# Attention and expert layer on one core: dividing by the softmax sums in the transposed layout, gate columns beside the values' weights, queries and keys laid out by direct copies

## The reference

```python
x = L0_attn_x                                   # (4, 512, 256) float32
# attention, 16 heads of 16, causal, no bias
qkv = (x @ w_qkv).reshape(b, s, 3, 16, 16)
q, k, v = qkv[:, :, 0] / 4, qkv[:, :, 1], qkv[:, :, 2]
scores = where(causal, einsum('bqhd,bkhd->bhqk', q, k), -1e10)
out = einsum('bhqk,bkhd->bqhd', softmax(scores), v).reshape(b, s, 256)
x = layernorm(x + out @ w_out)
# 32 experts, top 4 of each token
w4, i4 = top_k(softmax(x @ gate), 4); w4 = w4 / w4.sum()
for each token and each of its experts e:
    g, u = split(x @ gate_up[e])                # 2 x 96
    y += w4[e] * ((u * silu(g)) @ down[e])      # 96 -> 256
x = layernorm(x + y)
```

## Time and profile before

| what | us |
|---|---|
| median of the runs | 477.55 |
| lowest, highest | 477.39, 483.26 |
| span of the profiled execution | 420.8 |
| PE busy in the span | 377.7 (90%) |
| DVE busy | 287.1 (68%) |
| ACT busy | 242.4 (58%) |
| POOL busy | 235.4 (56%) |

### The profile page before, as it was taken

The page is one execution under the profiler, slowest core; times in us unless marked ns, Lnnn a source line. Parts: engine busy times, 40 slices in busy tenths (PEclk is TensorE's granted clock), DMA queues, the critical chain, the costliest instruction groups (busy, mean ns, idle before and its releaser), DMA issues.

```text
span 420.8 us, 10405 instructions
## 1 busy us (share of the span) xinstructions
PE 377.7 (90%) x2894; PEld 223.1 (53%) x2894; DVE 287.1 (68%) x1009; ACT 242.4 (58%) x534; POOL 235.4 (56%) x374
## 2 busy tenths in 40 slices
PE   5979999999999999997989899988999999989780
PEld 2526554444565445653444466665676777665230
DVE  1157767887879789889799489763666666643562
ACT  2431566667555776556857447562666666556842
POOL 5422144444223888227872855777777766646762
PEclk9999999999999999999999999996999999999987
DMA  4858555646751282649547435636655554429693
GB/s 137 261 192 231 172 165 173 189 136 209 213 164 29 90 277 91 190 144 276 176 149 224 138 123 149 189 132 195 188 175 169 165 158 145 129 69 369 235 375 118
DMA packets 54071, 74.78 MB, mean 178 GB/s; under 512 B 9842, under 2 KB 45308, under 8 KB 52480
## 3 DMA queue, kind: packets, MB, share of 16 engines
q1 hardware_dynamic: 46832, 56.93, 45.7%
q0 software_dynamic: 6912, 16.93, 11.0%
q10 hardware_dynamic: 272, 0.26, 0.2%
HBM read 46.33 MB, written 29.66 MB: 181 GB/s over the span
## 4 chain that ended last, share of the span: by engine, by line
PE 64%; DVE 16%; issue 7%; DMA 6%; ACT 3%; SPq 1%; POOL 1%; ACTq 0%; DVEq 0%
PE PS L697 12%; PE PS L868 8%; PE PS L719 7%; PE PS L821 6%; PE PS L790 5%; PE PS L847 5%; PE PS L665 5%; PE PS L804 3%; DVE MX L1425 2%; PE PS L928 2%; PE PS L710 2%; PE PS L898 2%; DMA YL<-scratch_y 2%; DMA scratch_qk<-PA 1%; DMA scratch_y<-Y,XG 1%
## 5 line engine op out<-in xcount | busy, mean ns | idle before, releaser
L1139 ACT ACTIVATE PT<-PS 128x512 f32<-128x512 f32 x160 | 92.0, 596 | 41.7 <-PE PS L847 36.9
L1783 POOL DMA_INDIRECT scratch_y<-Y,XG x80 | 79.5, 994 | 35.6 <-issue 18.2
L1755 POOL TENSOR_SCALAR_AFFINE_SELECT PT<-PT 128x256 f32<-128x256 f32 (+1 forms) x140 | 50.1, 367 | 78.0 <-ACT PT L1139 76.3
L1774 POOL DMA_INDIRECT scratch_slots<-XP,RI x64 | 63.8, 997 | 35.1 <-DVE XP L1368 16.1
L821 PE MATMUL PS<-KS,QS 96*128 96x512 bf16 (+3 forms) x256 | 61.7, 302 | 10.9 <-DVE MX L1432 4.6
L697 PE MATMUL PS<-W,XGT 128*64 x320 | 61.8, 337 | 1.2 <-DVE WG L1289 0.7
L847 PE MATMUL PS<-QS,KS 98*128 98x512 bf16 (+3 forms) x256 | 60.9, 299 | 1.5 <-ACT PT L1139 1.5
L699 PE MATMUL PS<-WG,XGT 128*64 128x192 f32 x320 | 61.9, 338 | 0.0
L1353 DVE SCALAR_TENSOR_TENSOR HH<-PS,XG,SG 128x96 f32<-128x96 f32 x80 | 24.9, 316 | 35.7 <-ACT SG L1061 31.0
L697 PEld LDWEIGHTS PS<-W,XGT 128*64 128x64 f32 x320 | 41.2, 139 | 13.7 <-issue 9.0
L821 PEld LDWEIGHTS PS<-KS,QS 96*128 96x128 bf16 x256 | 21.4, 99 | 44.7 <-DVE MX L1432 16.7
(11 more groups left out here) (237 smaller groups left out, 718.3 us busy)
## 6 DMA issues: line engine op xcount, KB each, us to landing
XG<-scratch_slots SPq DMA_DIRECT2D x160, 65.0 KB
scratch_qk<-PA SPq DMA_DIRECT2D x14, 384.0 KB, 3.4
W<-in_gate_up_dram SPq DMA_DIRECT2D x16, 288.0 KB
KS<-scratch_qk SPq DMA_DIRECT2D x32, 128.0 KB, 3.5
YL<-scratch_y SPq DMA_DIRECT2D x8, 512.0 KB, 7.0
QS<-scratch_qk SPq DMA_DIRECT2D x8, 384.0 KB, 3.7
QS<-scratch_qk SPq DMA_DIRECT2D x24, 128.0 KB, 3.6
W<-in_down_dram SPq DMA_DIRECT2D x8, 288.0 KB
```

The source lines that it names most:

```text
L1139: e.activation(PT[:, p % NPT, n, :], PS[:, 2 + (rank[u] - 1) % 2, :], ACT.Exp).then_inc(st_exp, 1)
L1755: e.affine_select(out=d, in_=d, compare_op=ALU.is_ge, fill=0.0, base=0, pattern=[[0, 1 if n < 2 else 2], [1, 128]], channel_multiplier=-1) ...
L1774: e.indirect_dma_start(out=XS[:, :], out_offset=bass.IndirectOffsetOnAxis(ap=RI[:, b % 2, TOPK * q + n:TOPK * q + n + 1], axis=0), in_=XP[ ...
L1783: e.indirect_dma_start(out=YK[:, :], out_offset=bass.IndirectOffsetOnAxis(ap=XG[:, j % NXG, D + 1:D + 2].bitcast(I32), axis=0), in_=Y[:, j ...
```

## The change

- Queries and keys: "qkout", "load" and the DRAM tensor go. A unit "lay" copies each piece directly from `PA` to its rows of QS or KS, six DMAs of 128 KB on SP. The "qk" units of sequences 1 to 3 stand at slots 20g-18 and 20g-12 of their group g; before, those of sequence 1 stood ahead of slot 17.
- The gate's columns are appended to the values' weights. A "v" unit takes 128 tokens with 288 columns; ACT copies V and XL from the same bank. "xg" and the tile `GT` with its load go.
- Values and ones alternate in V's tile, so that even rows of RAW are output and odd rows sums. Unit "spread" copies the even partitions of RAW to `AT` and the odd ones to `SU`, two DMAs of 64 partitions, on SP, and for the last quad on ACT. "norm" goes with its transposes. "att" becomes work of DVE alone: reciprocal of SU (128x512) and AT times SU in place.
- On SP at the start the ones and sequence 1's transposed X stand behind the copies of all four "qk" units of sequence 0.
- Fillers of PE in the last chain: 8, 8, 3 and 14 instead of 3, 4, 3 and 14.

```diff
-QS_ROWS = ((0, 2, 3, 0), (1, 6, 1, 1), (3, 6, 1, 1), (5, 6, 1, 2))
-KS_ROWS = ((0, 3, 2, 1), (1, 6, 1, 0), (2, 6, 1, 0), (5, 6, 1, 0), (4, 6, 1, 2))
+TERMS = 6
+QS_TERMS = ((0, 2, 4), (1, 3), (5,))
+KS_TERMS = ((1, 2, 5), (0, 3), (4,))
...
-            put(slot + 3, ("qkout",) + u[1:])
+            put(slot + 3, ("lay",) + u[1:])
...
-        elif u[0] == "norm" and u[2] % 2:
-            put(slot + 3, ("att", u[1], u[2] // 2))
+        elif u[0] == "spread" and u[1] % 2:
+            put(slot + 4, ("att", u[1] // 4, u[1] // 2 % 2))
         elif u[0] == "att" and u[2]:
-            put(slot + 3, ("proj", u[1], 0))
+            put(slot + 2, ("proj", u[1], 0))
...
-            plan += [("load", 0), ("v", 0, 0), ("v", 0, 1)]
+            plan += [("v", 0, q) for q in range(4)]
             for m in (1, 3):
-                plan += [(kind, 0, m) for kind in ("qk", "resid", "part", "qkout")]
+                plan += [(kind, 0, m) for kind in ("qk", "resid", "part", "lay")]
+            plan += [("ones",), ("xt", 1)]
         else:
...
+            for q in range(4):
+                put(5 + 2 * q if b == 1 else VALUES_AT[b - 2] + 2 * q, ("v", b, q))
+            for half in range(2):
+                put(20 * (2 * b + half) - 18, ("qk", b, half))
+                put(20 * (2 * b + half) - 12, ("qk", b, 2 + half))
...
-                put(slot + 3, ("norm", b, n))
+                put(slot + 1, ("spread", g))
...
+        def spread(e, g):
+
+            b, c, r = g // 4, g // 2 % 2, g % 2
+            e.wait_ge(raw_out, g + 1)
+            if b:
+                e.wait_ge(*full(("proj", b - 1, 3)))
+            for tile, first in ((AT, 0), (SU, 1)):
+                e.dma_start(tile[64 * r:64 * r + 64, c, :], RAW[first:128:2, r, :]).then_inc(spread_in[r], 16)
...
+                elif kind == "lay":
                     b, m = a
+                    g = 2 * b + m % 2
+                    r, rows = (rank[u] - 1) % 2, (KS if m >= 2 else QS)[g % RG]
                     wait_st_group(e, g - RG)
+                    for n, part in enumerate((part0, part1, part2)):
+                        e.wait_ge(part, rank["qk", b, m])
+                        for t in (KS_TERMS if m >= 2 else QS_TERMS)[n]:
+                            e.dma_start(rows[t:TERMS * HD:TERMS, :, :], PA[:, r, n, :]).then_inc(laid(b, m)[0], 16)
...
-            idle = {("norm", B - 1, 3): 3, ("att", B - 1, 1): 4, ("proj", B - 1, 0): 3, ("place", B - 1): 14}
+            idle = {("spread", QUADS - 1): 8, ("att", B - 1, 1): 8, ("proj", B - 1, 0): 3, ("place", B - 1): 14}
...
-                elif kind == "norm":
-                    b, n = a
-                    r = n % 2
-                    heads = PS[:, k, :].rearrange("p (x d) -> p x d", d=2 * HD)
-                    e.wait_ge(*full(u))
-                    e.reciprocal(SM[:, r, :].unsqueeze(2), heads[:, :, HD:HD + 1]).then_inc(sum_recip, 1)
-                    if b:
-                        e.wait_ge(*full(("att", b - 1, n // 2)))
+                elif kind == "att":
+                    b, c = a
+                    for r in range(2):
+                        e.wait_ge(spread_in[r], 32 * rank[u])
+                    e.reciprocal(SU[:, c, :], SU[:, c, :]).then_inc(sum_recip, 1)
                     e.wait_ge(sum_recip, rank[u])
...
+                    e.tensor_tensor(AT[:, c, :], AT[:, c, :], SU[:, c, :], ALU.mult).then_inc(att_out, 1)
...
-            e.memset(V[0][:, :, :, HD:2 * HD], 1.0)
-            e.memset(V[1][:, :, :, HD:2 * HD], 1.0).then_inc(consts, 1)
+            e.memset(V[0][:, :, :, 1:2 * HD:2], 1.0)
+            e.memset(V[1][:, :, :, 1:2 * HD:2], 1.0).then_inc(consts, 1)
```

More of the change, by code:

```diff
@@ L60 @@
 READY = {name: n + 1 for n, name in enumerate(CONSTS)}
-MISC = ("qk", "v", "xg", "wot", "wog", "sendmax", "norm", "att", "proj", "place", "count", "ends",
+MISC = ("qk", "v", "wot", "wog", "sendmax", "proj", "place", "count", "ends",
         "ecount", "eends", "etable", "lcount", "lends", "ltable")
+VG = D + NE
 def make_plan():
-    plan = [("inputs",), ("xt", 1)]
+    plan = [("inputs",)]
     rows, placed = [], set()
@@ L157, in make_plan @@
     put(27, ("wog",))
-    for b in range(1, B):
-        put(5 * (8 * b - 2) + 4 if b == 1 else VALUES_AT[b - 2] + 5, ("xg", b))
     for lo, n, slot in WEIGHTS:
         put(slot, ("w", lo, n))
-    for g in range(2, 2 * B):
-        put(5 * (4 * g - 3), ("load", g))
     for g in range(PAIRS // 2):
@@ L216, in one, with build @@
         return 1
[L219 removed]
+def build(nc, x, xt, w_qk, w_v, w_out, gup, dwn, out):
     ctx = ExitStack()
@@ L361, in build @@
         n_misc = 0
-        waiting = None
         for u in plan:
-            assert waiting in (None, u) or u[0] not in MISC, "another unit between a unit's halves"
-            waiting = u[1:] if u[0] == "half" else None if u == waiting else waiting
             kinds[u[0]] = kinds.get(u[0], 0) + 1
@@ L766, in _ @@
                     keep_busy(idle[u])
-                whole = u[1:] if kind == "half" else u
-                what, a = whole[0], whole[1:]
-                parts = (0,) if kind == "half" else ((1,) if ("half",) + u in rank else (0, 1))
-                if what in MISC:
-                    k = 6 + bank[whole][0]
-                    done = misc_full[bank[whole][0]]
+                if kind in MISC:
+                    k = 6 + bank[u][0]
+                    done = misc_full[bank[u][0]]
                 if u == ("open", 0):
@@ L924, in _ @@
                     e.wait_ge(*free(("wog",)))
-                    for c in range(2):
-                        e.wait_ge(*free(("att", b, c)))
+                    e.wait_ge(att_out, 2 * b + 2)
                     for c in range(2):
@@ L1105, in rows_out_early @@
                              ACT.Copy).then_inc(xgt_out, 1)
+            order = [u[1:] for u in plan if u[0] == "qk"]
             table_set()
```

205 lines of the change are left out of this document (60 added, 145 removed).

## The result

| | before | after |
|---|---|---|
| median of the runs, us | 478.7 | 520.39 (518.11 to 523.76) |
| ratio to before, 95% interval | 1 | 1.0833 [1.0754, 1.0912] |
| span of the profiled execution, us | 420.8 | 517.5 |

The account below looks back on a forecast made before the run. PE was taken as the bound, with DVE having only 30 us idle. Terms -8.6 + 21.6 - 2 + 1 - 1.2 + 2.6 = +13.4 us on 477.55 us gave 491 us, range 474 to 502 us.

Parts of the forecast that it names:

- slot 20 against before (start): Start of the attention: earlier first maxima offset by the late load of sequence 1, +1 us (-3 to +4).
- reciprocal of 128x512: DVE in each att: 3.2 us by extending the small reciprocals' line; lower bound 0.69 us.
- PE stands behind the six blocks: Attention window: six att blocks of 3.9 us on DVE each stop PE for 3.6 us, +21.6 us.
- relief of PE's other waits: Attention window: lighter DVE elsewhere, without 13 norms, takes back some of PE's waits, -2 us (0 to -5).
- PE work in the window: Attention window: removed transposes and gate units less wider values' products and moved qk units, -8.6 us (-9.6 to -5).
- rest of the window: Attention window: added transfers, ACT's copies and qk units' side work on other engines, costed at nothing.
- drain and last chain: After the last maxima: drain -1.2 us (-2 to +3), last chain from RAW to projection +2.6 us.
- its bound of +4: Start: upper bound, +4 us, if idle PE comes back at the lower clock level and SP is later still.
- Rival 4: Start: direct layout brings nothing measurable; undisturbed 3 us less, 488 us. Chance 0.60 together with the forecast.
- 1: Rival on DVE: the wide reciprocal runs at one element per cycle, blocks cost 6.6 us, 473 us. Chance 0.10.
- 2: Rival in the window: DVE's 30 us of idle time take up the blocks, 469 us. Chance 0.12.
- 3: Rival on SP's queue: late RAW copies make DVE wait, 5 x 2 us, or the start loses that; 501 us. Chance 0.18.

Follow-up runs that it names:

- e7: Kernel before with only the gate columns put behind the values' weights and no separate gate unit: ratio 0.990.
- e10: Kernel before with six unused 128x512 reciprocals on DVE and twelve filler products of PE behind each: ratio 1.051.
- e6: Changed kernel with the normalisation of before and sequence 1's transposed X loaded early; direct copies, new slots and gate columns stay: ratio 1.003.
- e5: Changed kernel with sequence 1's transposed X loaded early and the reciprocal on ACT as exp(-ln(x)): ratio 1.020.
- e4: Changed kernel itself, run again on one chip with e5, e6 and e7: 524.13 us, ratio 1.082 to the kernel before.
- e1: Changed kernel with only the load of sequence 1's transposed X moved back to its early place: ratio 1.077.
- e2: Changed kernel with only the reciprocal moved from DVE to ACT, as exp(-ln(x)): ratio 1.068.
- e13: Same as e6, but with sequence 1's transposed X loaded late again, behind sequence 0's copies and the ones: ratio 1.026.
- e0: Kernel before, unchanged, profiled again: 423.91 us, span 422.2 us.
- e3: Kernel before with six 128x512 reciprocals added on DVE at the att units of sequences 0 to 2, results unused: ratio 1.061.
- e9: Kernel before with the six added reciprocals of e3 each cut into four 128x128 pieces in slots of their own: ratio 1.062.

## Why the prediction was wrong

The direction was right, the size was not: 491 us with a range to 502, against 520. By its own steps:

| step | forecast | measured |
|---|---|---|
| slot 20 against before (start) | +1 | +0.7 (46.0 against 45.3) |
| reciprocal of 128x512 | 3.2 us | 3.35 us |
| PE stands behind the six blocks | 21.6 | 18.2 |
| relief of PE's other waits | -2 | +1.3 (10.3 against 9.0) |
| PE work in the window | -8.6 | busy +11.8 |
| rest of the window | 0 | +3.1, of which 2.9 the stop ahead of the last maxima |
| drain and last chain | +1.4 | some +5 |

**The reciprocal was right, and the stalls nearly.** A stall is 3.0 us in the mean, not 3.6, and the relief did not come; that the two together give +19.5 where 19.6 was forecast is luck. The small reciprocals read as a line gave the wide one: 3345 ns mean, of which 158 ns fixed leave 6.2 ns an element. "VectorE: DVE Perf Modes" of the Trainium skill, section "First, the fixed hardware budget", gives a repeat count of 8 for Reciprocal. The measured row has 6.2 ns an element where a plain operation has 1.04, six times as much, and decides.

**The step that failed is the PE work term.** The prediction counted what was removed at the durations of the earlier trace rows, all of them at a granted clock of 1.00, and left the clock where it was: PE busy would have been 162.1 - 8.6 = 153.5 us. It was 173.9 us. Of those 20.4 us some 16 to 19 are the same instructions at the lower level part of the time: the five lines of unchanged work grew by 16.4 us, and the clock of 0.91 over 206.4 us gives 18.6 us of lost clock, an estimate from another column. The other 2 to 4 us are work mis-sized at full clock, as in e7: overlapping products were taken out at their full rows, and the wider ones cost 1.7 us more, not 1.0. The prediction knew of the two levels only at the start (its bound of +4). That the stalls of 3.6 us it put into the window would take the clock with them was not in any term, and its range to 502 us had no room for it. e10 shows the mechanism in isolation, in the kernel before: 10 us of PE's busy time and 6.5 us of the window for six blocks. That the changed kernel's PE has nearly twice this on it is not taken apart further, and fillers were not tried in it, so how much of its 206.4 us a full clock would give back is not shown. It has more stops: e6, without any block, stands at 0.97, e5 with DMA copies at 0.94, e4 at 0.89. "TensorE: Matmul & The Clock Gate" of the Trainium skill, section "HAM oscillation — how this bites in real kernels", describes this for waits on DMA: they make each burst of TensorE begin at the low clock. The trace agrees that a stop brings the low clock, with 0.61 us a product instead of 0.38 behind it, but not that the burst begins with it: the first products behind the stop at 85.30 us still take 0.39. The page would have named the missing term.

**A stop that no term had.** In the change each sequence's projections follow its last "att" sooner, and with them the choice of the experts. For the third sequence this brings 3.9 us of DVE work (247.79 to 251.71 us) ahead of the last maxima, where it stood behind them before. PE waits 4.31 us for them instead of 1.42. Every trace with the new normalisation has this stop (4.3 us in e1, e2, e4 and e5), and e6 and e13 don't (1.4).

**The late load was forecast rightly and valued wrongly.** Rival 4 said that undisturbed the direct layout would be 3 us better. e13 against e6 gives 10 to 12 us. The forecast of +1 against before held only because the direct copies' head start, and four "qk" units put off behind slot 20, paid for it.

**PE work removed is not always time removed.** Gate columns alone: 3.4 us of PE in the window, 5.1 us of time (e7). But e6, with all of the PE savings except the transposes, gains nothing: its window is 13.3 us longer than e7's. Of this 9.7 us is PE busy time, 5.9 of them the three moved units and the rest mostly the clock of 0.97, and 3.6 us are waits: 2.8 us of them for residuals of "qk" units on DVE, which the prediction had put at nothing. The direct layout in its full form loses what it saves.

**Drain and last chain.** From pair 31 to the last sequence's first projection e0 takes 25.1 us and e1, the changed kernel but for the load, 30.4 us on the same chip; on that of e4 to e7 it is 47.0 us in e4 against 41.9 in e7 and 43.3 in e6: +4 to +5 where +1.4 was forecast. In the last chain the copy of SU is issued at 289.72 us and DVE starts at 293.05; RAW to projection takes 8.7 us where 4.8 stood before (+3.9, forecast +2.6): the DMA took 3.3 us from issue to landing where the earlier trace rows had 1.8.

**The rivals.** 1 falls (3.35 us). 2 falls (e3, and e9 for short pieces too). 3 does not appear in the window: DVE waits for RAW's copies 21.1 us in all, but 20.1 us of it is the last chain, where it has nothing else to do. 4 is above.

**The account**, from runs and their windows: gate columns -5 us (e7); direct copies and slots, load early, +5 (e6 less e7); late load +10 to +13 (e13, e5); normalisation by DMA with the reciprocal elsewhere +8 (e5's 492.8 less e6's 484.99 us); reciprocals on DVE instead of ACT +16 (e4 less e5 in the window). The sum, +34 to +37, stands beside +38.9 measured on that chip and +39.9 in the result. By it the six reciprocals are the largest part and cost less than forecast; the late load, the copies and the moved units are what the forecast had near nothing, and the lower clock runs through all of them.

**What stays open.** Which part of the +8 of e5, beyond the 2.9 us ahead of the last maxima, is ACT's work, which the product on DVE and which late DMAs; why the chips differ behind the attention, where on the slow one PE, DVE and ACT do nothing from 235 to 240 us (e7) while POOL goes on; and how much of the 16 to 19 us of clock belongs to each kind of stop.

## What to carry to other kernels

Where two engines hand two buffers back and forth, as PE and DVE do here, take an operation put on one of them at its whole duration, whole or cut in pieces, whatever idle time the table of windows shows for that engine. If it makes TensorE stand, add the clock: in e3 the window grew by 27% more than the blocks' own time, and in the changed kernel unchanged work of PE took 16 us longer. And judge a layout by the stage's end, not by its start: work that is put off makes a start look early.

## What the runs showed of the hardware

- A reciprocal on DVE costs 6.2 ns an element: 250 ns for 128x16, 952 ns for 128x128, 3350 ns for 128x512, whether float32 or bf16. The product of the same 128x512 takes 693 ns, so dividing costs five times as much as multiplying; the small form before, 16 times 250 ns, did the same job in 4.0 us where the wide one takes 26.8 us.
- The same program differs by 13 to 15% between chips (421, 423, 423, 479, 485 us for the kernel before), and nearly all of the difference lies behind the last maximum: e6 and e13, on a slow and a fast chip, have windows within 0.2 us of each other and need 43.3 and 25.4 us from there to the last sequence's first projection.
- After a stop of PE the clock can fall late: behind the 3.85 us ahead of 85.30 us the first products still took 0.39 us, and from 86.5 to 89.6 us the granted clock was 0.50.
- Copies of 128 KB from SBUF to SBUF land 2.4 us after their issue (median of 48 each for queries and keys), where the store to DRAM, with a fetch still to follow, took 1.8 us.
